# A decoder layer on one core: probabilities times values in three fp32r passes, with VectorE's mixing step one iteration later and its low-part step directly behind the row maximum

## The reference

```python
normed = _rmsnorm(hidden_states, norm_w)
v_pool = jnp.concatenate([normed, memory_state], axis=1)
q = jnp.einsum('bsh,oh->bso', normed, q_w)
k = jnp.einsum('bth,oh->bto', v_pool, k_w)
logits = jnp.einsum('bsd,btd->bst', q, k) * scale      # causal on the sequence, all of the context
attn = jax.nn.softmax(logits, axis=-1)
h_tilde = jnp.einsum('bst,bth->bsh', attn, v_pool)
alpha = jax.nn.sigmoid(jnp.einsum('bsh,oh->bso', hidden_states, gate_w) + gate_b)
return (1.0 - alpha) * hidden_states + alpha * h_tilde
```

## Time and profile before

| | |
|---|---|
| median of 3 runs | 571.68 us (571.42 to 571.88) |
| profiled execution: its own time, and the span in the trace | 574.74 us, 572.9 us |
| busy: PE, DVE, ACT, POOL | 543.2, 456.9, 329.9, 344.8 us (95, 80, 58, 60% of the span) |
| chain that ended last | PE 77%, DVE 5%, issue 4%, ACT 4%, POOL 2% |
| mean granted TensorE clock | 0.985 |

### The profile page before, as it was taken

How to read it: one execution, slowest core, us unless ns; L and a number is a source line. 1 busy time by engine, 2 the same in 40 slices (tenths; PEclk the granted TensorE clock), 3 DMA queues, 4 the chain that set the end, 5 groups by cost and what they waited for, 6 DMA issues and landing times.

```text
span 572.9 us, 10819 instructions
## 1 busy us (share of the span) xinstructions
PE 543.2 (95%) x3156; PEld 477.2 (83%) x3156; DVE 456.9 (80%) x1163; ACT 329.9 (58%) x742; POOL 344.8 (60%) x470
## 2 busy tenths in 40 slices
PE   4997999999999999999999888999999999999986
PEld 4876888888888888888888766899999999999976
DVE  3587679767798757977578567999999999999984
ACT  4335652737446375462653656777777777777651
POOL 4024928449276384582679527777777777777640
PEclk9998999999999999999999998999999999999998
DMA  8620400000000000000000000000000000000001
GB/s 233 187 76 8 146 2 0 2 2 0 0 0 0 0 1 1 2 1 1 1 1 1 1 1 1 10 19 18 18 18 18 18 19 26 18 18 18 20 19 37
DMA packets 16124, 13.78 MB, mean 24 GB/s; under 512 B 3883, under 2 KB 15839, under 8 KB 16095
## 3 DMA queue, kind: packets, MB, share of 16 engines
q1 hardware_dynamic: 16095, 13.43, 7.7%
HBM read 9.23 MB, written 4.19 MB: 23 GB/s over the span
## 4 chain that ended last, share of the span: by engine, by line
PE 77%; DVE 5%; issue 4%; ACT 4%; POOL 2%; DVEq 0%; ACTq 0%; POOLq 0%
PE ps L892 17%; PE ps L894 17%; PE ps L893 17%; PE ps L1090 9%; PE ps L1233 4%; PE ps L1078 2%; PE ps L1010 2%; PE ps L1011 2%; PE ps L1088 2%; PE ps L1126 1%; PE ps L982 1%; ACT xn_sums L631 1%; DVE nT_l L1308 1%; PE ps L1019 1%; PE ps L1076 1%
## 5 line engine op out<-in xcount | busy, mean ns | idle before, releaser
L892 PE MATMUL ps<-keys_h,nT_h 128*128 128x256 f32 (+6 forms) x304 | 95.1, 313 | 1.9 <-DVE keys_l L1308 1.5
L893 PE MATMUL ps<-keys_l,nT_h 128*128 128x256 f32 (+6 forms) x304 | 92.5, 304 | 0.0
L894 PE MATMUL ps<-keys_h,nT_l 128*128 128x256 f32 (+6 forms) x304 | 92.3, 304 | 0.0
L892 PE MATMUL ps<-parts,xq_parts 128*128 128x512 f32 (+1 forms) x192 | 78.8, 411 | 4.3 <-DVE xq_parts L1491 4.2
L894 PE MATMUL ps<-parts,xq_parts 128*128 128x512 f32 (+1 forms) x192 | 73.4, 382 | 0.0
L893 PE MATMUL ps<-parts,xq_parts 128*128 128x512 f32 (+1 forms) x192 | 72.6, 378 | 0.0
L1090 PE MATMUL ps<-V,probT 128*128 128x256 f32 x288 | 68.5, 383 | 0.0
L674 ACT ACTIVATE prob<-ps,nbias 128x205 f32<-128x205 f32 (+7 forms) x32 | 25.7, 804 | 70.9 <-DVE nbias L1388 70.9
L892 PEld LDWEIGHTS ps<-keys_h,nT_h 128*128 128x128 f32 x304 | 57.8, 190 | 6.1 <-issue 1.9
L1090 PEld LDWEIGHTS ps<-V,probT 128*128 128x128 f32 x288 | 55.4, 193 | 8.1
L893 PEld LDWEIGHTS ps<-keys_l,nT_h 128*128 128x128 f32 x304 | 57.7, 190 | 3.4
(11 more groups left out here) (217 smaller groups left out, 1537.6 us busy)
## 6 DMA issues: line engine op xcount, KB each, us to landing
X<-in_x_dram SPq DMA_DIRECT2D x8, 512.0 KB, 5.3
out_dram<-X SPq DMA_DIRECT2D x32, 128.0 KB, 1.7
early<-in_L_ffn_w_down_dram SPq DMA_DIRECT2D x1, 704.0 KB, 7.0
early<-in_L_ffn_w_gate_dram SPq DMA_DIRECT2D x1, 640.0 KB, 4.4
early<-in_L_ffn_w_up_dram SPq DMA_DIRECT2D x1, 640.0 KB, 5.6
ctx_rows<-in_ctx_dram SPq DMA_DIRECT2D x1, 308.0 KB
early<-in_L_attn_Winv_dram SPq DMA_DIRECT2D x1, 256.0 KB, 3.9
early<-in_L_attn_WQ_dram SPq DMA_DIRECT2D x1, 256.0 KB, 5.1
```

What stands on the lines that cost most here:

```text
L892: mm(o, wh, mh, start=start, stop=False, **kw)
L893: mm(o, wh, ml, start=False, stop=False, **kw)
L894: return mm(o, wl, mh, start=False, stop=stop, **kw)
```

## The change

The products of `pv_tile` with `V` become three fp32r passes. For this

- ACT copies transposed probabilities to `probT_h` (fp32r; the context block stays fp32 as `probT_c`), and DVE makes `probT_l` in a new `turn_low`, from the same PSUM banks. PE's `turn_tile` now waits for `s_probT_l` before it reuses a bank, and the third chunk of tile 7 moves behind `y_half(b + 1, 1)`.
- POOL writes the values in place over `nrm`, ACT makes `V_h` in a new `values_high` (one instruction for four tiles), and POOL makes `V_l` in a new `values_low` (one instruction for a tile). `sum_half(b + 1, 0)` and `values_half(b + 1, 0)` stand at the end of POOL's batch.
- DVE's iteration i is now `max_tile(i)`, `mix_tile(i - 3)`, `x1_half` (i = 5), `turn_low(i - 1)`, and then the rest; `mix_tile(7)` stays in iteration 9. In iteration 8 `x1_half(b + 1, 1)` and `keys_low(b + 1, 0)` stand behind `mix_tile(5)`.
- Room is made: `hid` holds 4 tiles for 8, `gz` goes (the gate's sum is written to `th`), `scanA` shares space with `xn`, and `zE` with `inv_row`. ACT's `hid_half(b + 1, 0)` moves from iteration 6 to the end of iteration 8.

The core of the diff:

```diff
@@ POOL
+            def values_low(b, h):
+                q = b * 2 + h
+                pool.wait_ge(s_V_h, q + 1)
+                for i in range(h * HALF, (h + 1) * HALF):
+                    g.tensor_tensor(V_l[:, i, :], nrm[:, i, :], V_h.bitcast(F32)[:, i, :], ALU.subtract).then_inc(s_V, 1)
...
             def batch(b, more, ahead=False):
-                sum_half(b, 0)
-                values_half(b, 1)
+                values_low(b, 0)
                 base_tiles(b, (0, 1))
                 base_tiles(b, (2, 3))
+                values_half(b, 1)
                 sum_half(b, 1)
+                values_low(b, 1)
@@ ACT
+            def values_high(b, h):
+                c = slice(h * HALF, (h + 1) * HALF)
+                act.wait_ge(s_values, b * 2 + (h + 1))
+                act.wait_ge(s_pv, START + b * TPB)
+                a.activation(V_h[:, c, :], nrm[:, c, :], ACT.Copy).then_inc(s_V_h, 1)
...
                     for t in GATES[i]:
                         gate_tile(b, t)
+                    if i == 0:
+                        values_high(b, 0)
                     if i == 1:
                         keys_half(b, 1)
                     if i == 3:
                         hid_half(b, 1)
+                        values_high(b, 1)
@@ PE
                 for m in range(1, i + 2):
-                    last = mm(ps[:, 5, 0:D], probT[:, i % 2, m, :], V[:, m - 1, :], start=False, stop=(m == i + 1))
+                    last = mm_parts(ps[:, 5, 0:D], (probT_h[:, i % 2, m - 1, :], probT_l[:, i % 2, m - 1, :]),
+                                    (V_h[:, m - 1, :], V_l[:, m - 1, :]), start=False, stop=(m == i + 1))
@@ DVE
+            def turn_low(b, i, which=(0, 1, 2)):
+                for c, blocks in enumerate(chunks[i]):
+                    if c not in which:
+                        continue
+                    k = chunk0[i] + c
+                    bank, m0, m1 = 3 + k % 2, max(blocks[0], 1), blocks[-1] + 1
+                    ve.wait_ge(s_probT, START + b * CPB + (k + 1))
+                    if i >= 2:
+                        ve.wait_ge(s_pv, START + b * TPB + (i - 1))
+                    low(probT_l[:, i % 2, m0 - 1:m1 - 1, :],
+                        ps[:, bank, (m0 - blocks[0]) * P:(m1 - blocks[0]) * P].rearrange("p (m n) -> p m n", n=P),
+                        probT_h[:, i % 2, m0 - 1:m1 - 1, :]).then_inc(s_probT_l, 1)
...
                 for i in range(TPB + 2):
                     if 1 <= i < TPB:
                         max_tile(b, i)
+                    if i >= 3:
+                        mix_tile(b, i - 3)
+                    if more and i == 5:
+                        x1_half(b + 1, 0)
+                    if 1 <= i < TPB:
+                        turn_low(b, i - 1)
+                    if i == TPB:
+                        turn_low(b, TPB - 1, (0, 1))
+                    if not more and i == TPB:
+                        turn_low(b, TPB - 1, (2,))
                     if more:
                         if i == 4:
                             tri_half(b * 2 + 2, 0)
-                        if i == 5:
-                            x1_half(b + 1, 0)
...
-                    if i >= 2:
+                    if i == TPB + 1:
                         mix_tile(b, i - 2)
```

More of the change, by code:

```diff
@@ L125, in decoder_layer @@
         keys_h, keys_l = (sb(n, [P, KD, OWN + S], F32R) for n in ("keys_h", "keys_l"))
-        V = sb("V", [P, TPB, D])
-        hid = sb("hid", [P, TPB, D])
-        gz = sb("gz", [P, 2, D])
+        V_h, V_l = (sb(n, [P, TPB, D], F32R) for n in ("V_h", "V_l"))
+        hid = sb("hid", [P, HALF, D])
         th = sb("th", [P, HALF, D])
@@ L207, in decoder_layer @@
         sg, hh, hy = (over(prob, 3, I)[:, k, :] for k in range(3))
-        hmag, ht = (over(probT, 2, I)[:, k, :] for k in range(2))
-        hq_wide = over(probT, 2 * I + KI * P)[:, 2 * I:2 * I + KI * P]
+        hmag, ht = (raw[:, k * I:(k + 1) * I] for k in range(2))
+        hq_wide = raw[:, 2 * I:2 * I + KI * P]
         hq = hq_wide[:, 0:I]
@@ L213, in decoder_layer @@
         xsq, xm = (xmag.bitcast(BF16)[:, k * D:(k + 1) * D] for k in range(2))
-        xq = dmix[:, 2, :]
+        xq = dmix[:, 1, :]
         xh = (xh0, xh1)
@@ L469, in sum_half @@
                 for i in range(h * HALF, (h + 1) * HALF):
-                    last = g.tensor_tensor(X[:, b * TPB + i, :], X[:, b * TPB + i, :], hid[:, i, :], ALU.add)
+                    last = g.tensor_tensor(X[:, b * TPB + i, :], X[:, b * TPB + i, :], hid[:, i % HALF, :], ALU.add)
                 last.then_inc(s_sum, 1)
@@ L546, in _ @@
             pool.wait_ge(w_in[3], 16 * 6)
+            sum_half(0, 0)
             values_half(0, 0)
@@ L1280, in _ @@
             v = nc.vector
-            for s_ in (s_mix1, s_out_ready):
+            for s_ in (s_mix1, s_out_ready, s_probT_l):
                 v.sem_inc(s_, START)
@@ L1332, in ctx_keys_low, with scan @@
                 low(keys_l[:, :, PAD:OWN], ctx_keys[:, :, bass.ds(b * C, C)], keys_h[:, :, PAD:OWN]).then_inc(s_ctx_keys_l, 1)
-            def scan(q, h, o, bank, k):
+            def scan(q, h, o, bank, k, b=None):
                 ve.wait_ge(s_proj, q * 4 + k)
-                start = o[:, HTOK - 1:HTOK] if h else 0.0
+                start = (last_sum_bi[:, 0:1] if o is scanA else o[:, HTOK - 1:HTOK]) if h else 0.0
+                if h and o is scanA:
+                    ve.wait_ge(s_bi_carried, q // 2 + 1 if isinstance(q, int) else b + 1)
                 v.tensor_tensor_scan(o[:, :], ones[:].broadcast_to([P, HTOK]), ps[:, bank, :], start, ALU.mult,
@@ L1341, in bi_half @@
             def bi_half(b, q, h, bank=6):
-                scan(q, h, scanA, bank, 1)
+                scan(q, h, scanA, bank, 1, b)
                 ve.wait_ge(s_proj, q * 4 + 2)
```

83 lines of the change are left out of this document (47 added, 36 removed).

## The result

The changed kernel takes 602.41 us (median of 4 runs, 602.25 to 605.13) against 571.61 us (571.42 to 571.88) for the kernel before on the same chip: a ratio of 1.0529, 95% interval 1.0490 to 1.0568. The forecast was 602. An interval of this kind reaches about 2.3 us to either side.

What follows compares the result with a forecast made beforehand. PE was taken as the bound, without slack. Three batches lose 25 us and the last 4, gain counted, plus 2 for the clock: 602 us median, 604 for a profile's span. Range 580 to 616.

Steps and rivals of the forecast that it cites:

- Gain on PE: Products with V: three fp32r passes take 0.35 us a block for 0.43, saving 2.95 us a batch, 11.8 in all.
- Wait 1: End of a batch with a next one: PE's tile 7 product waits for tile 6's mixing behind `keys_low`; 2.2 us, three times.
- Wait 2: Iterations 0 to 2: `V_h` and tile 0's low part delay gates, `xn_half` and PE's transposes; 1.8 us a batch, last 1.4.
- Wait 3: Iteration 3: tile 1's product waits for tile 0's mixing, now behind tile 3's maximum; 1.2 us in each of four batches.
- Wait 4: Inner stretch, logits 4 to `keys_products`: DVE's queue becomes longer than PE's; 4 us net, 1 to 5.5.
- Last batch: Sum for the last batch: 1.4 + 1.2 + 3 less about 1.5 saved, a loss of 4 us.
- The clock: PE's waits bring half-clock stretches, each costing at most 1.7 us; 2 us in all, 10 as upper end.
- The small loss: Rival: DVE's work fits the inner stretch, whose added wait is about 1 us; 590 or 584 us, chance 0.14.
- That PE stays the bound: Rival: exponentials come earlier and at most the wait before tile 7's product remains; 566.5 or 560 us, chance 0.07.
- The clock rival: Each batch loses two or three half-clock stretches on the path; about 612 us, chance 0.14 shared with dearer passes.
- The rival of dearer passes: Three passes cost over 0.35 us as weights change each block, at most 0.43; +11.8 us, chance 0.14 shared with clock.
- The rule on the shared port: POOL's 32 new subtractions could each block a DVE mixing addition up to 0.76 us; half hit gives 602 + 6.

Runs made afterwards that it cites:

- the run with one fp32 product: Changed kernel with one fp32 product of the high parts in place of the three passes with V: 607.67 us, 1.0608.
- the run with one pass: Changed kernel making only the first (high by high) of the three passes of probabilities times values: 606.08 us, 1.0579.
- mixing 6: Changed kernel with DVE mixing tile 6 in iteration 8, ahead of `keys_low` of the next batch: 605.58 us, 1.0581.
- mixing 0: Changed kernel with DVE mixing tile 0 at the end of iteration 2, ahead of the maximum of tile 3: 606.01 us, 1.0586.
- `norm1_half`: Changed kernel with both `norm1_half` of the batch after next moved from iterations 5 and 7 to iteration 9: 606.49 us, 1.0579.
- The five moves together: Changed kernel with tiles 6 and 0 mixed earlier, gates 2 and 3 before tile 0's low part, `V_h` early, `norm1_half` in iteration 9, `rstd_half` behind `values_half`: 583.05 us, 1.0162.

## Why the prediction was right, by its own steps

- **Gain on PE.** Starts of a block's first pass are 208.66 - 208.31 = 0.35 us apart, as predicted. But a product's first block takes 208.31 - 207.77 = 0.54, since its first pass, behind the fp32 product with the context rows, takes 0.30 and not 0.12. The kernel before shows the same where fp32r followed fp32 (its logits behind the products of tile 7: 0.29 us at 202.75), so this is new only where an fp32 operation comes next, three times a batch in the loop (tiles 0, 3 and 5). The gain was put a little too large: the run with one fp32 product adds 2.6 us to PE's busy time in batch 1, for 2.95. It costs 5.3 us, so under this order about half of the saving is on the path. PE's busy time fell by 6.7 us from before to after, with 3.0 us more at half clock.
- **Added work.** Low parts 27.1 us (15.0 + 5.5 + 3.3 + 3.3) for 28; 384 columns 0.546 for 0.55; `V_h` 1.05 for 1.1. No wait of PE is released by POOL, as put.
- **Wait 1**: 2.08 for 2.2. Taken away, it gave 2.7 us up to the start of batch 1, which the next iterations took back.
- **Wait 2**: 2.00 and 1.89 in batches 1 and 2, against 0.38 and 0.29 before, so 1.6 twice for 1.8. In batch 0 it was 3.00. The chain is the one described; each half of it can be shortened by itself.
- **Wait 3**: 1.08 and 1.00 for 1.2, in all four batches.
- **Wait 4**: the inner stretch of batch 1 grew from 45.77 to 48.69, 2.9 us net for 4. DVE is busy for 43.70 of 48.69 us, 90%, and PE's waits there carry DVE's lines. The dead time ahead of the maximum of tile 7 and the contention at mixing tile 3 were mis-sized by parts: DVE waits 1.79 us at the first (0.75 before), 1.0 more for 1.5, and the addition at the second took 0.43, so the 1 us put there did not come in this batch; in batch 2 it did: the addition at 266.56 took 2.20 us, with a POOL operation of 1120 columns beside it from 265.86. The prediction also left out what goes: the additions that took 1.82 and 1.12 us in batch 1 before take at most 0.89 now. In batch 2, without `norm1_half`, the waits of the stretch are 1.23 and 0.77.
- **The batches.** 8.3 us for each of three was 11.0, 7.4 and 4.4: nearly the same sum (22.8 for 25) from unequal parts. The first holds two stretches at half clock more than before and the wait of 3.00; the third has less on DVE.
- **Last batch**: 6.7 us for 4. This term was too small: the products of tiles 2 to 5 wait 0.54, 1.60, 0.37 and 2.39 us, 4.9 in sum, of which I took 3 net, and logits 3 wait 1.97 us, 1.6 more than before (0.40), for 1.4.

```profile
312.27 0.48 PE L914 MATMUL ps<-keys_h,nT_h 128*128 128x462 f32 x1 [1.97 <-ACT prob L693]
...
350.74 0.70 PE L1111 MATMUL ps<-ctx_rows,probT_c 77*128 77x256 f32 x2 [2.39 <-DVE dmix L1441]
```

- **The clock**: 20.5 us at half clock within the span for 17.5, so at most 1.5 us of PE's time for 2. The exact hit at 602 is in part luck: the batches miss by 2.7, -0.9, -3.9 and 2.7 us, which nearly cancel, and for a profile's span the forecast was 604, where 600.4 was measured. The medians meet it to half a microsecond only because the traced execution of before lay 3.1 us over its median.
- **Rivals.** The small loss (584 to 590) is what the same instructions reach in another order (583.1, 582.5), so 19 us of the loss were not a matter of DVE's capacity but of the order that the code has. For the 11 us that stay, and for the 11.8 us less of products that bring nothing there, no run shows the cause. That PE stays the bound is refuted by the run with one pass. The clock rival did not come in after; in the run with one pass, half clock and longer waits together eat the gain. The rival of dearer passes holds for each product's first block alone.
- **The rule on the shared port** (the Trainium skill, SBUF — State Buffer, Who interferes with whom) would have put 6 us on the subtractions. Without them the mixing additions took 1.3 us less in all, and the time did not fall. Here POOL's subtractions seldom lie beside those additions: in the trace of after at 4 of 32.

What stays open: single moves whose wait is gone in the trace (mixing 6, mixing 0, `norm1_half`) come out at or above after's time. The traces show longer waits on ACT's chain in the first and the last of these (3.0 us for 2.0), and the executions of the three have a granted clock of 0.969 to 0.983, after's 0.983 to 0.986; the two haven't been separated. The five moves together are worth 19.4 us; which pairs are needed was not tried. No order tried beats the kernel before.

## What to carry to other kernels

Before an engine's work is shortened, ask which queue is next: here a 33.7 us cut on the busiest engine gave nothing, and reordering gave 19 us. Cost an inserted step by what stands behind it in its own queue and who waits for that, and move all steps of a chain together, since a wait removed alone comes back at the next link. A low part that must follow a copy on another engine belongs behind whatever that other engine will need next.

## What the runs showed of the hardware

- The clock halves behind short waits, not only behind long ones. The wait of 3.08 us at 182.15 in the run with one pass has the clock falling while PE still stands, and the stretch is over before 186. A 2.25 us wait at 154.21 in the same run is followed by the fall within the transposes behind it, but the 2.00 and 2.08 us waits of batch 1 in after are not: that batch has a clock of 1.00. So a wait of 2 us may or may not cost up to 1.7 us more, half of a stretch of 3.4 us.
- Less work on TensorE came with more time at half clock (58.3 us for 20.5) and more idle time (85.1 us for 63.9).
- A TensorE pass in fp32r behind an fp32 product took 0.30 us to the next start, the passes behind it 0.12.
- A DVE subtraction out of PSUM costs 0.28, 0.42, 0.55 and 0.68 us for 128, 256, 384 and 512 columns.
